# Delta rule on one core: factors of 16 builds made ahead in small pieces, later solves and squares, and centred key weights

## The reference

```
kvx = einsum('bsi,oi->bso', cond, w_kv_x);  kx, vx = split(kvx)
kx = _ln(kx.reshape(b, sc, g, d), kxln_w, kxln_b)      # (x - mean) * rsqrt(var + 1e-5)
```

```
g = cumsum(g);  decay = exp(g[i] - g[j]) for i >= j
A = -(k_beta @ k.T) * decay, strictly lower;   attn = inv(I - A)
v_new = attn @ v_beta;   o = (q @ k.T * decay) @ v_new        # q, k scaled to unit length
```

## Time and profile before

| | us |
|---|---|
| median of 3 runs | 2781.6 (2780.59 to 2783.29) |
| the profiled execution | 2779.4 |
| its span | 2777.6 |
| cross-attention batches, about | 200 to 1850 |
| projections of the delta rule, about | 1866 to 2192 |
| recurrence | 2192.7 to 2362 |
| output projection and experts | 2362 to 2777 |

### The profile page before, as it was taken

The page is one execution under the profiler, slowest core; times in us unless marked ns, Lnnn a source line. Parts: engine busy times, 40 slices in busy tenths (PEclk is TensorE's granted clock), DMA queues, the critical chain, the costliest instruction groups (busy, mean ns, idle before and its releaser), DMA issues.

```text
span 2777.6 us, 39649 instructions
## 1 busy us (share of the span) xinstructions
PE 2646.0 (95%) x13810; PEld 2194.4 (79%) x13810; DVE 1861.7 (67%) x4737; ACT 1574.0 (57%) x2992; POOL 504.8 (18%) x428
## 2 busy tenths in 40 slices
PE   6889999999999999999999999999999879999999
PEld 5778788887887887887887887878877768777887
DVE  7747648548547557457466476668669866668997
ACT  7945436436436445445345355437676567857776
POOL 4402002002002012011011020005353332022111
PEclk9989999999999999999999999999999999989999
DMA  3433013022022031031030121445676642549996
GB/s 125 137 123 86 10 55 93 15 67 75 17 79 61 20 88 46 24 94 30 24 99 20 40 84 50 132 140 156 177 211 168 158 94 66 187 184 368 376 371 228
DMA packets 255061, 317.91 MB, mean 114 GB/s; under 512 B 128712, under 2 KB 166216, under 8 KB 241808
## 3 DMA queue, kind: packets, MB, share of 16 engines
q1 hardware_dynamic: 251392, 310.03, 36.0%
q0 software_dynamic: 3040, 5.08, 0.7%
q10 hardware_dynamic: 432, 0.27, 0.0%
HBM read 274.22 MB, written 46.98 MB: 116 GB/s over the span
## 4 chain that ended last, share of the span: by engine, by line
PE 79%; DVE 10%; ACT 4%; issue 2%; DMA 2%; POOL 1%; SPq 1%; POOLq 0%; DVEq 0%; ACTq 0%
PE ps L103 20%; PE ps L105 20%; PE ps L104 20%; PE ps L874 3%; PE ps L830 3%; PE ps L902 2%; DVE lnw L2169 2%; DVE zz L2172 2%; PE ps L855 1%; DVE cv L2136 1%; PE ps L895 1%; PE ps L1344 1%; PE ps L1343 1%; PE ps L2010 1%; PE ps L579 1%
## 5 line engine op out<-in xcount | busy, mean ns | idle before, releaser
L1244 POOL TENSOR_TENSOR lnw<-lnw,half 128x8 f32<-128x8 f32 x88 | 144.4, 1641 | 1217.6 <-DVE lnw L964 1217.6
L103 PE MATMUL ps<-whf,cth 128*128 128x512 f32 (+1 forms) x832 | 336.1, 404 | 1.8 <-ACT kn L1117 1.8
L103 PE MATMUL ps<-cnh,pth 128*128 128x512 f32 (+1 forms) x832 | 329.9, 397 | 6.4 <-issue 6.4
L105 PE MATMUL ps<-whf,ctl 128*128 128x512 f32 (+1 forms) x832 | 325.9, 392 | 0.0
L104 PE MATMUL ps<-cnl,pth 128*128 128x512 f32 (+1 forms) x832 | 324.9, 390 | 0.0
L104 PE MATMUL ps<-wlf,cth 128*128 128x512 f32 (+1 forms) x832 | 324.9, 390 | 0.0
L105 PE MATMUL ps<-cnh,ptl 128*128 128x512 f32 (+1 forms) x832 | 324.6, 390 | 0.0
L2662 DVE TENSOR_TENSOR ml<-mr,mh 128x2048 fp32r<-128x2048 f32 x90 | 203.3, 2286 | 26.5 <-ACT mh L2604 26.5
L1155 ACT ACTIVATE pr<-ps,sm 128x1601 f32<-128x1601 f32 x56 | 89.6, 1600 | 205.7 <-DVE sm L1017 205.7
L1180 ACT ACTIVATE xo<-ps 128x128 f32<-128x128 f32 x64 | 17.7, 277 | 312.9 <-PE ps L902 312.9
L1036 DVE TENSOR_TENSOR ptl<-ps,pth 128x512 fp32r<-128x512 f32 (+1 forms) x256 | 139.1, 585 | 78.8 <-ACT pth L1167 78.4
(11 more groups left out here) (349 smaller groups left out, 6421.5 us busy)
## 6 DMA issues: line engine op xcount, KB each, us to landing
mr<-in_moe SPq DMA_DIRECT2D x90, 1024.0 KB, 7.2
ctr<-in_ctxt SPq DMA_DIRECT2D x96, 256.0 KB, 3.0
pr<-in_ctxn SPq DMA_DIRECT2D x96, 256.0 KB
wv<-in_wv SPq DMA_DIRECT2D x64, 256.0 KB, 2.8
wr<-in_wqkv SPq DMA_DIRECT2D x64, 256.0 KB, 3.0
wvf<-in_wattn SPq DMA_DIRECT2D x11, 1024.0 KB, 4.9
ca<-cat_d SPq DMA_DIRECT2D x16, 512.0 KB, 3.9
qk_d<-cv SPq DMA_DIRECT2D x32, 256.0 KB, 3.3
```

Source lines behind the costliest of these rows:

```text
L103: pe.matmul(dst, lh, rh, start=first, stop=False)
L105: return pe.matmul(dst, ll, rh, start=False, stop=last)
L1244: po.tensor_tensor(rs[0:w, s, :], nv[0:w, s, :], half[0:w, 0:8], ALU.pow).then_inc(kx_rs, 1)
```

## The change

**Centred key weights.** DVE subtracts from each chunk of wkr its mean over each group of 128 outputs (`center_wk_dv`: a reduction and a scalar_tensor_tensor of 128x1024), and ACT's wkh waits for it. The projected keys then have mean zero, so the norm needs only the scale: bn_aggr is replaced by four small operations on all groups, nmr and its semaphore go, ACT copies with a scale, and DVE norms four groups in one product.

**Factors ahead.** For builds 16 to 31 the rows of g, beta and now rq (transposed with them; gb_d has three rows per head) come in four pieces of 16 heads. Between the places 39 and 89 SP loads a piece, POOL masks it (four additions of 128x512), ACT takes one exponential, POOL scales (four more, so that beta holds beta times decay and the decay holds rq), and SP stores it to cf_d. The builds then load finished factors in rows of 4 KB. The decay step and POOL's three instructions per build go; the coupling becomes two dependent products of 128 columns; p3 of n >= 16 needs no scale. The clear of mt and xt moves from place 38 to place 91.

**Order.** Two builds per step up to t=3, other budgets, solve 1 wholly in t=0, solve 2 from t=6, solve 3 from t=17, "system 2" in t=4. Squares: groups 0 to 7 every second step from t=8, the others two per step from t=24, in one ACT instruction, summed by one DVE reduction.

```diff
-        gb_d = dram("gb_d", [128, 2, 128])
+        gb_d = dram("gb_d", [2, 128, 3, 64])
+        cf_d = dram("cf_d", [4, 128, 2048])
...
+        def center_wk_dv(dv, c):
+
+            raw = wkr[:, c, :].rearrange("p (g d) -> p g d", g=8)
+            if c == 0:
+                dv.wait_ge(d_wv, 16)
+            t = vs(dv.tensor_reduce(mv[:, c, :, 0], raw, AX.X, ALU.add))
+            dv.wait_ge(dv_step, t)
+            dv.scalar_tensor_tensor(raw, mv[:, c, :, 0].unsqueeze(2).to_broadcast([128, 8, 128]), -1.0 / 128.0, raw,
+                                    ALU.mult, ALU.add).then_inc(wk_centered.sem, 1)
...
                     self_max_dv(dv, k + 3)
+                if k == 0:
+                    center_wk_dv(dv, 0)
                 if 1 <= k < 5:
+                    if k < 4:
+                        center_wk_dv(dv, k)
...
-                    if k == 0:
-                        ac.wait_ge(d_wv, 16)
+                    ac.wait_ge(*wk_centered.at(k + 1))
...
+            apart, square = mv[0:w, s, lo:hi, 0], mv[0:w, s, lo:hi, 1]
+            dv.wait_ge(dv_step, t)
+            t = vs(dv.tensor_tensor(apart, bns[0:w, s, lo:hi, 1], bns[0:w, s, lo:hi, 4], ALU.subtract))
+            vs(dv.scalar_tensor_tensor(nv[0:w, s, lo:hi], bns[0:w, s, lo:hi, 2], 128.0 * 1e-5, bns[0:w, s, lo:hi, 5],
+                                       ALU.add, ALU.add))
+            dv.wait_ge(dv_step, t)
+            t = vs(dv.scalar_tensor_tensor(square, apart, 0.25, apart, ALU.mult, ALU.mult))
+            dv.wait_ge(dv_step, t)
+            dv.scalar_tensor_tensor(nv[0:w, s, lo:hi], nv[0:w, s, lo:hi], 1.0 / 128.0, square, ALU.mult, ALU.add).then_inc(kx_var, 1)
...
-            for g in range(4, 8):
-                f = dv.tensor_scalar(dst[0:w, g, :], src[:, 128 * g:128 * g + 128], mv[0:w, s, g, 0:1],
-                                     rs[0:w, s, g:g + 1], ALU.subtract, ALU.mult)
-            f.then_inc(kn_dv, 1)
+            dv.tensor_tensor(dst[0:w, 4:8, :], src[:, 512:1024].rearrange("p (g d) -> p g d", g=4),
+                             rs[0:w, s, 4:8].unsqueeze(2).to_broadcast([w, 4, 128]), ALU.mult).then_inc(kn_dv, 1)
...
-            ac.wait_ge(kx_nm, n + 1)
+            ac.wait_ge(kx_rs, kx_stat_of(n, 0))
             kn_free(ac, n)
             for g in range(4):
-                f = ac.activation(dst[0:w, g, :], src[:, 128 * g:128 * g + 128], ACT.Identity,
-                                  scale=rs[0:w, s, g:g + 1], bias=nmr[0:w, s, g:g + 1])
+                f = ac.activation(dst[0:w, g, :], src[:, 128 * g:128 * g + 128], ACT.Copy, scale=rs[0:w, s, g:g + 1])
...
+        ALONE = 8
+
+        def on_ac(n):
+            return n < 20
...
-                yield "decay", n, 0
...
+                for k, (first, mask, scale) in enumerate(((39, 46, 49), (52, 57, 64), (67, 73, 76), (79, 84, 87))):
+                    if first <= s < first + 4:
+                        yield "pg_load", k, s - first
+                    if s in (mask, mask + 1):
+                        yield "pg_mask", k, s - mask
+                    if s == mask + 2:
+                        yield "pg_exp", k, 0
+                    if s in (scale, scale + 1):
+                        yield "pg_scale", k, s - scale
+                    if s == scale + 2:
+                        yield "pg_store", k, 0
+                if s == 91:
+                    yield "clear", 0, 0
...
-                yield from some(steps, 400 if t < 3 else 700)
+                yield from some(steps, 500 if t < 12 else 700)
                 if 0 <= t - 1 < 32:
                     yield "p1", t - 1, 0
-                for _ in range(2 if t < 3 else 1):
+                for _ in range(2 if t < 4 else 1):
                     if todo:
                         yield from building(todo.pop(0))
-                if t == 13:
+                if t == 12:
                     yield from built()
                 if 0 <= t - 2 < 32:
                     yield "p2", t - 2, 0
-                yield from some(steps, 400 if t < 3 else 800 if t < 15 else 1000)
+                yield from some(steps, 400 if t < 12 else 800)
                 if 0 <= t - 3 < 32:
                     yield "p3", t - 3, 0
-                if t in (4, 14, 22):
+                if t in (0, 14, 22):
                     yield from steps
-                    solved_to = (4, 14, 22).index(t) + 1
+                    solved_to = (0, 14, 22).index(t) + 1
                     yield "solved", solved_to, 0
-                if t in (6, 15):
-                    steps = solving(2 if t == 6 else 3)
+                if t in (5, 16):
+                    steps = solving(2 if t == 5 else 3)
                 while fetched < 16 and 2 * fetched <= t + 3 and fetched // 4 <= solved_to:
                     yield "fetch", fetched, 0
                     fetched += 1
-                if t in (5, 14):
+                if t in (4, 14):
                     yield "system", solved_to + 1, 0
                 if t >= 2 and t % 2 == 0 and t // 2 + 1 < 16:
                     yield "fetch_coupling", t // 2 + 1, 0
-                if squares <= t - 4 and squares < 28:
-                    yield "square", squares, 0
-                    squares += 1
-                    if squares % 2 == 0:
-                        yield "rms", squares // 2 - 1, 0
+                for _ in range(2 if t >= 24 else 1 if 8 <= t and t % 2 == 0 else 0):
+                    if squares < 28:
+                        yield "square", squares, 0
+                        squares += 1
+                        if squares % 2 == 0:
+                            yield "rms", squares // 2 - 1, 0
...
+            if m >= 8:
+                sp.wait_ge(*d_cf.at(16 * ((m - 8) // 2 + 1)))
             for b in range(2):
-                sp.dma_start((gb2 if core_over(m) else gb)[64 * b:64 * b + 64, f:f + 2, :, :, :].rearrange("p f h a t -> p (f h) a t"),
-                             gb_d[8 * m:8 * m + 8, :, 64 * b:64 * b + 64].unsqueeze(0).to_broadcast([64, 8, 2, 64])).then_inc(d_gb[m % 4].sem, 16)
+                dst = (gb2 if core_over(m) else gb)[64 * b:64 * b + 64, f:f + 2, :, :, :]
+                if m >= 8:
+                    sp.dma_start(dst.rearrange("p f h a t -> p (f h a t)"),
+                                 cf_d[(m - 8) // 2, 64 * b:64 * b + 64, 1024 * (m % 2):1024 * (m % 2) + 1024]).then_inc(d_gb[m % 4].sem, 16)
+                else:
+                    sp.dma_start(dst.rearrange("p f h a t -> p (f h) (a t)"),
+                                 gb_d[b, 8 * m:8 * m + 8, 0:2, :].rearrange("h a t -> h (a t)").unsqueeze(0).to_broadcast([64, 8, 128])).then_inc(d_gb[m % 4].sem, 16)
+
+        def factor_load(sp, k, part):
+
+            sp.wait_ge(d_gt, 32)
+            if k > 0:
+                sp.wait_ge(*d_cf.at(16 * k))
+            h, row = 4 * part, 64 + 16 * k + 4 * part
+            for b in range(2):
+                sp.dma_start(pg[64 * b:64 * b + 64, h:h + 4, :, :].rearrange("p h a t -> p (h a t)"),
+                             gb_d[b, row:row + 4].rearrange("h a t -> (h a t)").unsqueeze(0).to_broadcast([64, 768])).then_inc(d_pg.sem, 16)
+
+        def factor_store(sp, k):
+            sp.wait_ge(*pg_scaled.at(4 * k + 4))
+            sp.dma_start(cf_d[k].rearrange("p (h c) -> p h c", h=16),
+                         pg[:, :, 0:2, :].rearrange("p h a t -> p h (a t)")).then_inc(d_cf.sem, 16)
...
+                elif step == "pg_exp":
+                    ac.wait_ge(*pg_masked.at(8 * n + 8))
+                    ac.activation(pg[:, :, 0, :], pg[:, :, 0, :], ACT.Exp).then_inc(pg_exp.sem, 1)
...
-                    for q in range(4):
-                        f = ac.activation(vb[:, j, h + q, :], bank(3 + n % 5)[:, 128 * q:128 * q + 128], ACT.Copy,
-                                          scale=rq[:, j, h + q:h + q + 1])
+                    if n < 16:
+                        for q in range(4):
+                            f = ac.activation(vb[:, j, h + q, :], bank(3 + n % 5)[:, 128 * q:128 * q + 128], ACT.Copy,
+                                              scale=rq[:, j, h + q:h + q + 1])
+                    else:
+                        f = ac.activation(vb[:, j, h:h + 4, :], bank(3 + n % 5).rearrange("p (h d) -> p h d", h=4), ACT.Copy)
...
+                        ac.activation(gz[:, n % 3, :].rearrange("p (h d) -> p h d", h=4), vb[:, n // 8, hd:hd + 4, :],
+                                      ACT.Square).then_inc(o_squared.sem, 1)
...
+                elif step == "pg_mask":
+                    e = pg[:, 8 * k:8 * k + 8, 0, :]
+                    po.wait_ge(*d_pg.at(128 * (n + 1)))
+                    po.tensor_tensor(e, e, negm.unsqueeze(1).to_broadcast([128, 8, 64]), ALU.add).then_inc(pg_masked.sem, 2)
+                    m = 4 * n + 2 * k
+                    po.wait_ge(*pg_masked.at(8 * n + 4 * k + 2))
+                    po.tensor_tensor(e, e, ngc[:, 2 + m // 8, 4 * (m % 8):4 * (m % 8) + 8].unsqueeze(2).to_broadcast([128, 8, 64]),
```

(27 more changed lines are left out.)

93 lines of the change are left out of this document (48 added, 45 removed).

## The result

The changed kernel takes 2788.1 us (median of 17 runs, 2781.6 to 2792.1), the kernel before in the same rounds 2780.0 (17 runs, 2777.3 to 2783.3): a ratio of 1.0029, 95% interval 1.0023 to 1.0036. It is slower by 8 us where 10.8 were forecast as gain. The profiled execution took 2786.8 us with a span of 2785.0.

The account below looks back on a forecast made before the run. PE, busy 95% of the span, was taken as the bound, DVE in some stretches. Terms -18 + 6.5 + 7.7 - 7 = -10.8 us took the profiled 2779.4 to 2768.6, plus 2.2 for the median: 2771 us, range 2755 to 2787.

Parts of the forecast that it names:

- The self-attention: Self-attention: DVE's four added centrings, 9.6 us in all, release turn 5 at 191.7 instead of 184.0; loss 7.7 us.
- The batches: Further 103 tiles: shorter norms and no wait for nmr save PE waits at batch ends; gain 7 us, range 0 to 8.
- (a): Recurrence, end of solve 1: DVE's last 20 small instructions run without POOL's factor work beside them; gain 5 us.
- (b): Recurrence, from 2204.5 to solve 2's start: 38.3 us shrink through shorter DVE and PE lines; gain 10 us, bounds 0 to 14.
- (c): Recurrence, solve 2 and its neighbours: 41 us become 38 under the new budgets; gain 3 us, range 0 to 6.
- (e): Recurrence, t=14 to 24 and the late squares: chained as before, 44 us against 43.5, extra DVE work hidden; gain nothing.
- POOL's term: Projections: 20.8 of POOL's 42 us fall in DVE's full stretches and lengthen half its work; loss 6 us, 0 to 13.5.
- ACT's table loads: Projections: four exponentials with two table loads each, 14.4 us of ACT, mostly in gaps; loss 1 us, range 0 to 4.
- DMA: Projections: 6.3 MB of gate rows and 4 MB of stores added, 256-byte pieces dropped; -0.5 us, range -3 to 5.
- slower: Rival, projections: SP waits for each piece's store and weight chunks with it, 22 us more; 2793 us, chance 0.1.
- shared path: Rival, projections: moved POOL work costs DVE nearly its full length, 13.5 us; recurrence gains 15; 2781 us, chance 0.16.
- The signs of being right: Self-attention reductions some 8 us later, no 0.9 us batch gaps, 0.3 us solve 1 steps, recurrence about 151 us without table loads.

Follow-up runs that it names:

- c_only: The kernel before with the centred key weights and their shorter statistics and norms alone: median 2775.2 us, ratio 0.9987 to the kernel before.
- after: The changed kernel with the whole change, against the kernel before: median 2788.1 us, ratio 1.0029.
- half: The changed kernel with factors ahead for builds 16 to 23 alone, groups at places 39 to 50 and 79 to 88: median 2774.2 us, ratio 0.9989.
- half_mid: The changed kernel with factors ahead for builds 16 to 23 alone, groups at places 52 to 66 and 67 to 78: median 2779.1 us, ratio 0.9996.

## Why the prediction was wrong

**The self-attention** was forecast at +7.7 and measured +8.1. The reason holds, DVE's queue is full there and gets four times 2.43 us, but the number is in part luck. The turn that the text follows by hand (183.96 before, forecast 191.7) came at 195.72, 11.8 us later: PE lost more than DVE's 9.7, its clock in the first stretch fell to 0.83 from 1.00. Behind it "what follows it stays" failed the other way, as PE ran two of the last three products of values at full clock (1.68 us for 3.06), which gave 3.5 us back.

**The batches** gave 11.7 for 7. The two gaps named did go: PE's "issue" at the batch ends fell from 6.4 us in 7 to 1.4 in 7, and that for ACT's kn (1.8) is gone, 6.8 in all for the text's 6.7. The rest: in the whole stage PE's idle time fell by 7.4 us (25.8 to 18.4) and the busy time of the same 8388 products by 4.2 (1634.6 to 1630.3). Why the products got shorter wasn't found; it is not a wait. The row after and the row before:

```profile
PE ps L104 <- issue: 1.4, 7, 0.2
```

```profile
PE ps L103 <- issue: 6.4, 7, 0.9
```

**The recurrence** was right in sum (16.2 for 18) and nearly by term: (a) solve 1 ends 5.2 us after p0(0) instead of 11.8, with steps of 0.36 to 0.19 us, so 6.6 for 5; (b) from there to solve 2's first step 30.3 us instead of 38.3, 8.0 for 10; (c) from solve 2's start to solve 3's 47.6 instead of 51.9, 4.3 for 3; (e) from there to the last p3 71.4 instead of 68.7, a loss of 2.7 for nothing. The rows:

```profile
2219.59 0.19 DVE L2262 TENSOR_TENSOR zz<-zz,lnw 128x31 f32<-128x31 f32 x1
...
2250.05 0.21 DVE L2259 TENSOR_TENSOR lnw<-cv,zz 128x31 f32<-128x31 f32 x1 [5.67 <-DMA cv<-at_d]
...
2297.62 0.21 DVE L2259 TENSOR_TENSOR lnw<-cv,zz 128x31 f32<-128x31 f32 x1
```

What the text credits to the order in (b) and (c) ("System 2" sooner, new budgets) the order alone did not bring: without the factors ahead its recurrence is no shorter than c_only's.

**The projections** are where the prediction failed, in the sum "6.5 lost, 0 to 20": 6 for POOL, 1 for ACT's tables, -0.5 for DMA. Measured were 22.4 us against c_only. The term that failed first is POOL's, "20.8 x 0.5 x 0.65 = 6.8 us, of which I count 6": the runs give it 8 us with the table loads there (351.0 to 342.8) and 15 with them away (351.5 to 336.3). The other two were sized too small as well, and all three were added as if none changed the price of another.

Two things were wrong in POOL's term. It let only half of POOL's 42 us count, those in the two stretches where DVE was nearly full in the kernel before. But PE's first product of each place, held against the kernel before, falls back in jumps from the first group on: 2.5 us at places 49 to 51, 3.0 at 59, 5.7 at 61 and 62, 2.4 at 67, 1.8 at 75, 4.7 at 78 and 2.3 at 92 and 93; 11.2 of the 23.5 us are lost before place 63. The rate itself was about right: 0.5 x 0.65 is 0.33 us of DVE's time for one of POOL's, and DVE took 14.8 us longer with POOL's 41.6 us of products than without (268.9 and 254.1), 0.36. (The 0.65 has no source in the text.) And it took DVE's lengthening for the whole loss: after each of the longer waits PE ran at its low clock, and its busy time grew by 8.3 us (324.7 against 316.4) of the 22.4.

**ACT's table loads** were put at 1, range 0 to 4, "in a stage where it has gaps". Their price depends on who else is late: nothing in after, 6.5 to 8.4 us once POOL's part is gone. The further 11 us that the text mentions for ACT don't show: before each of the stage's 20 table loads ACT is idle 0.02 us, and behind 16 of them the next instruction starts within 0.01. **DMA** was put at -0.5, range -3 to 5: 1.6 (all else there) to 4.7 (all else away) as measured, 3.9 to 7.0 with the estimate above, so at or past the upper end. **SP's wait** for the stores, the rival "slower", was 6.9 us in three waits, the longest 2.5; no wait of PE names a chunk or a store, the late chunks reach it through ACT.

The rival "shared path" had the mechanism (the lock, POOL's whole length), and its 13.5 us are near DVE's 14.8, though by another count: two thirds of 20.8 us, where the runs show a third of 41.6. It had nothing for the tables and the loads. Of the signs of being wrong the first came true, "the projections (1866 to 2194) longer by over 10 us"; solve 2 started 32.4 us after p1(0), within the 34. The signs of being right, all in the other stages, came true too, with 154.4 us of recurrence for 151.

## What to carry to other kernels

Work moved to an idle engine is priced by what it does to the engine that shares its path to SBUF. Where VectorE's instructions have two SBUF inputs, count every GpSimd instruction that reads SBUF at up to its full length on VectorE's side (here 14.8 us for 41.6 in sum), over all of the stage and not only where VectorE was full before. Put such work where VectorE has slack (half against half_mid: the same work, projections 8 us apart in one trace each, medians 5 us) or in a form that only writes. Never put at the head of an in-order queue a wait for a load that is itself issued behind that queue's output. And take pieces out in pairs: a single removal can show nothing for a cost of 6 us when another engine is late at the same place. Look too at what the removal itself adds: here the clearing of a tile, at some 2.3 us, hid over half of what the loads cost.
